# LSTM stage of a fused network kernel: one semaphore increment for two gates, input products four steps apart, more fillers ahead of the loop, and fillers on a 64x64 part of the array

## The reference, cut to what matters

```python
t = t + _L1_ffn_ref(_ln_t(t), ...)

def _L1_ffn_ref(x, U_i, V_i, b_i, U_f, V_f, b_f, U_c, V_c, b_c, U_o, V_o, b_o):
    B, T, _ = x.shape                       # 4, 256, 64
    xi = xt @ U_i + b_i                     # also xf, xg, xo
    def step(carry, xs):
        h, c = carry
        i_t = sigmoid(xi_t + h @ V_i)       # f_t is computed but not used below
        g_t = tanh(xg_t + h @ V_c)
        o_t = sigmoid(xo_t + h @ V_o)
        c_new = h * c + i_t * g_t
        h_new = o_t * tanh(c_new)
        return ((h_new, c_new), h_new)
```

## Time and profile before

| What | Value |
|---|---|
| Median of 3 runs | 818.9 us (811.82 to 820.67) |
| The profiled execution | 824.19 us |
| Its span, first to last instruction | 822.4 us |
| Mean granted TensorE clock | 0.80 of 2.4 GHz |
| TensorE matmul busy | 779.4 us (95%), fillers included |
| VectorE, ScalarE, GpSimd busy | 348.6, 231.5 and 123.0 us |

### The profile page before, as it was taken

One profiled execution on the slowest core, in us unless ns is written; L12 is line 12 of the kernel. 1 busy time (PEld: TensorE's weight loads), 2 busy tenths in 40 slices (PEclk: granted clock), 3 DMA queues, 4 the chain that ended last, 5 costly groups with the idle time before them and its releaser, 6 DMA issues.

```text
span 822.4 us, 17334 instructions
## 1 busy us (share of the span) xinstructions
PE 779.4 (95%) x7035; PEld 447.1 (54%) x7035; DVE 348.6 (42%) x1245; ACT 231.5 (28%) x1136; POOL 123.0 (15%) x148
## 2 busy tenths in 40 slices
PE   6898999999999999999898979999999999999998
PEld 3555555666556665555323745555555555555554
DVE  3444444433443334454655053444444444444443
ACT  2322222222222222213650012333333333333332
POOL 3333333333332223320000000000000000000000
PEclk8566666555655556658999987999999999999999
DMA  7000000000000000000000000000000000000000
GB/s 262 8 1 2 1 1 0 0 0 0 0 0 0 0 0 0 0 0 1 1 0 1 1 1 2 2 2 2 2 2 2 2 2 2 2 3 2 2 2 14
DMA packets 2994, 6.62 MB, mean 8 GB/s; under 512 B 1649, under 2 KB 2294, under 8 KB 2806
## 3 DMA queue, kind: packets, MB, share of 16 engines
q1 hardware_dynamic: 2934, 5.79, 2.1%
HBM read 5.52 MB, written 0.26 MB: 7 GB/s over the span
## 4 chain that ended last, share of the span: by engine, by line
PE 89%; DVE 8%; issue 1%; POOL 1%; ACT 1%; DVEq 0%; POOLq 0%; ACTq 0%
PE bk L668 26%; PE bk L315 15%; PE bk L648 11%; PE bk L427 4%; PE bk L606 3%; DVE a0y L923 2%; PE bk L642 2%; PE bk L534 2%; PE bk L437 2%; PE bk L552 2%; PE bk L379 2%; DVE hv L921 1%; PE bk L455 1%; PE bk L311 1%; PE bk L460 1%
## 5 line engine op out<-in xcount | busy, mean ns | idle before, releaser
L668 PE MATMUL bk<-idle 128*64 128x512 bf16 (+1 forms) x975 | 235.7, 363 | 0.0
L315 PE MATMUL bk<-idle 128*128 128x256 bf16 x608 | 147.3, 397 | 2.1 <-POOL lrcur L265 2.1
L648 PEld LDWEIGHTS bk<-mem,lvh 64*64 64x64 f32 x3072 | 80.9, 134 | 88.0 <-DVE mem L1093 83.7
L668 PEld LDWEIGHTS bk<-idle 128*64 128x64 bf16 x975 | 87.2, 110 | 57.7 <-issue 2.7
L1090 DVE TENSOR_TENSOR_SCAN bk<-gx 128x16 f32<-128x16 f32 x256 | 51.0, 199 | 131.9 <-ACT gx L820 131.9
L648 PE MATMUL bk<-mem,lvh 64*64 64x4 f32 x3072 | 103.4, 204 | 0.0
L820 ACT ACTIVATE gx<-bk 128x8 f32<-128x8 f32 x256 | 47.1, 184 | 178.1 <-PE bk L648 178.1
L315 PEld LDWEIGHTS bk<-idle 128*128 128x128 bf16 x608 | 67.4, 129 | 42.6 <-issue 11.5
L1093 DVE SCALAR_TENSOR_TENSOR mem<-og,bk 128x4 f32<-128x4 f32 x256 | 40.6, 158 | 57.4 <-ACT bk L824 57.4
L281 POOL TENSOR_TENSOR mem<-mem,gcur 128x1024 f32<-128x1024 f32 x16 | 30.3, 1892 | 212.6 <-DVE mem L950 212.3
L824 ACT ACTIVATE bk<-bk 128x4 f32<-128x4 f32 x256 | 40.4, 158 | 52.8 <-DVE bk L1090 52.0
(11 more groups left out here) (274 smaller groups left out, 857.3 us busy)
## 6 DMA issues: line engine op xcount, KB each, us to landing
cw<-in_cw SPq DMA_DIRECT2D x1, 3456.0 KB, 11.2
w<-in_w SPq DMA_DIRECT2D x2, 512.0 KB, 3.6
xs<-in_x SPq DMA_DIRECT2D x1, 256.0 KB, 2.6
out<-xs SPq DMA_DIRECT2D x1, 256.0 KB, 2.1
memw<-in_memw SPq DMA_DIRECT2D x1, 128.0 KB, 2.1
lu<-in_lu SPq DMA_DIRECT2D x1, 97.5 KB
wqkv<-in_wqkv SPq DMA_DIRECT2D x1, 96.0 KB, 2.2
lv<-in_lv SPq DMA_DIRECT2D x1, 96.0 KB
```

Source lines behind the costliest of these rows:

```text
L315: nc.tensor.matmul(bk[:, bank, 0:256], idle[:, 0:128], idle[:, 128:128 + 256], start=True, stop=True)
L648: return nc.tensor.matmul(bk[HALF[n], 3 * (s // CH % 2) + g, c:c + B], lvh[HALF[k], g, :], hist[HALF[k], s, :], start=False, stop=True, sk ...
L668: nc.tensor.matmul(bk[0:D, 7, 0:n], idle[:, 0:D], idle[:, 128:128 + n], start=True, stop=True)
```

## The change

What it does:

- TensorE signals gates_ig once per step, after the second of the two gates, and ScalarE waits for s + 1 in place of 2s + 2.
- The input products of the next chunk are issued in steps 2, 6 and 10 of a chunk in place of 2, 3 and 4. Such a step has two fillers of 512 columns and none of 256.
- The fillers between the steps use 64 rows by 64 output columns in place of 128 rows by 64.
- 39 fillers in place of 28 ahead of the transposes of xn, and six more (`AFTER[8]`, into bank 7) behind them.
- One signal after all eight transposes. VectorE copies bank 4 and ScalarE bank 5, the first half of the steps first; the loop starts when the first half is there, and the second half is waited for at chunk 7, step 2, ahead of the input products for chunk 8.

```diff
+INPUT_STEPS = (2, 6, 10)
...
-AFTER = (8, 14, 10, 4, 0, 20, 4, 28)
+AFTER = (8, 14, 10, 4, 0, 20, 4, 39, 6)
...
             busy(AFTER[7], 0)
             pe.wait_ge(sem("ln"), 3)
-            for n in range(NT):
-                ins = nc.tensor.transpose(bk[0:D, 4 + n // 4, (n % 4) * 128:(n % 4 + 1) * 128], xn[:, n, :], ident[:, :])
-                if n % 4 == 3:
-                    ins.then_inc(sem("t3T_ps"), 1)
+            for c in range(2):
+                for b in range(B):
+                    ins = nc.tensor.transpose(bk[0:D, 4 + b // 2, (b % 2 * 2 + c) * 128:(b % 2 * 2 + c + 1) * 128], xn[:, 2 * b + c, :], ident[:, :])
+            ins.then_inc(sem("t3T_ps"), 1)
+            busy(AFTER[8], 7)
             pe.wait_ge(sem("ld_l"), 32)
-            pe.wait_ge(sem("t3T"), 3)
+            pe.wait_ge(sem("t3T_a"), 1)
+            pe.wait_ge(sem("t3T_v"), 2)
...
                 recurrent(s, 0, 0, 0)
-                recurrent(s, 0, 0, 1).then_inc(sem("gates_ig"), 1)
+                recurrent(s, 0, 0, 1)
                 recurrent(s, 1, 1, 0)
                 recurrent(s, 1, 1, 1).then_inc(sem("gates_ig"), 1)
...
-                if 2 <= s % CH < 5 and s // CH + 1 < S // CH:
-                    inputs_part(s // CH + 1, s % CH - 2)
-                    fills = max(fills - 1, 0)
+                last = FILL_LAST
+                if s % CH in INPUT_STEPS and s // CH + 1 < S // CH:
+                    if (s // CH + 1) * CH == S // 2:
+                        pe.wait_ge(sem("t3T_a"), 2)
+                        pe.wait_ge(sem("t3T_v"), 3)
+                    inputs_part(s // CH + 1, INPUT_STEPS.index(s % CH))
+                    fills, last = FILL - 1, 0
                 if s + 1 < S:
-                    for n in [FILL_N] * fills + [FILL_LAST]:
-                        nc.tensor.matmul(bk[0:D, 7, 0:n], idle[:, 0:D], idle[:, 128:128 + n], start=True, stop=True)
+                    for n in [FILL_N] * fills + [last] * (last > 0):
+                        nc.tensor.matmul(bk[0:D, 7, 0:n], idle[0:D, 0:D], idle[0:D, 128:128 + n], start=True, stop=True)
...
             table(ACT.Tanh)
+            act.wait_ge(sem("t3T_ps"), 1)
+            for c in range(2):
+                nc.scalar.copy(
+                    t3T[0:D, c * 128:(c + 1) * 128, 2:4].rearrange("p s b -> p b s"),
+                    bk[0:D, 5, :].rearrange("p (b c s) -> p b c s", b=2, c=2)[:, :, c, :]).then_inc(sem("t3T_a"), 1)
...
-                act.wait_ge(sem("gates_ig"), 2 * s + 2)
+                act.wait_ge(sem("gates_ig"), s + 1)
...
-            for n in range(2):
-                dve.wait_ge(sem("t3T_ps"), n + 1)
-                for c in range(2):
-                    ins = nc.vector.tensor_copy(
-                        t3T[0:D, c * 128:(c + 1) * 128, 2 * n:2 * n + 2].rearrange("p s b -> p b s"),
-                        bk[0:D, 4 + n, :].rearrange("p (b c s) -> p b c s", b=2, c=2)[:, :, c, :])
-                ins.then_inc(sem("t3T"), 1)
+            dve.wait_ge(sem("t3T_ps"), 1)
+            for c in range(2):
+                nc.vector.tensor_copy(
+                    t3T[0:D, c * 128:(c + 1) * 128, 0:2].rearrange("p s b -> p b s"),
+                    bk[0:D, 4, :].rearrange("p (b c s) -> p b c s", b=2, c=2)[:, :, c, :]).then_inc(sem("t3T_v"), 1)
```

More of the change, by code:

```diff
@@ L1008, in _ @@
             nc.vector.tensor_copy(sel.rearrange("p (e m) -> p e m", e=E), wide(pick3[:, :], 128)).then_inc(sem("sel"), 1)
-            nc.vector.memset(t3T[D:D + 1, :, :], 1.0).then_inc(sem("t3T"), 1)
+            nc.vector.memset(t3T[D:D + 1, :, :], 1.0).then_inc(sem("t3T_v"), 1)
             dve.wait_ge(sem("ld_l"), 32)
```

## The result

The changed kernel takes 961.39 us (median of 4 runs, 958.39 to 965.46) against 819.78 us for the kernel before (4 runs): a ratio of 1.1754, 95% interval 1.1666 to 1.1842. It is slower by 17.5%, far outside the forecast range of 798 to 816. Some executions are a few us slower than the rest, whatever the kernel: ratios leave these out, medians do not.

The account below looks back on a forecast made before the run. The prediction took the chain of dependences to set ordinary steps and TensorE's queue the input steps, with a half-clock dip at the loop's start. Terms -0.7 - 6.9 - 4.6 = -12.2 took 818.9 to 806.7 us, range 798 to 816.

Parts of the forecast that it names:

- Fillers on 64x64. They stream the same columns: cost 0: Between the steps: fillers on 64 rows by 64 columns take the same time as 128-row ones, 0 us.
- the clock is lost with the quadrant: In the loop: 64-row fillers may not hold full clock; +228 us, about 1045 (about 930 if alternating); chance 0.11.
- The dip, -6.9: Start of the LSTM loop: with TensorE kept occupied, the 15.61 us at half clock become 8.69, so -6.9 us.
- the first rival: In the opening: the clock falls all the same, as transposes and small products do not keep it; 813.9 us, chance 0.14.
- The opening, -0.7: Ahead of the loop: copies and input products finish earlier, first recurrent products at 487.85 instead of 488.57, -0.7 us.
- The input steps, -4.6: 42 input steps at full clock: losing the 256-column filler saves 0.11 us each, 1.24 instead of 1.35, -4.6 us.
- One increment, 0: Weight load to ScalarE in each step: one semaphore increment in place of two, at most 0.04 us a step, taken as 0.
- The border between shapes: Filler to recurrent product: 0.12 us beyond what the columns need, removed if both are 64x64, only widening slack in ordinary steps.
- the last rival: Input steps cost more by the change of array shape, +0.12 us in each of 45, at most +5.4; 812.1 us, chance 0.08.

## Why the prediction was wrong, step by step

**"Fillers on 64x64. They stream the same columns: cost 0"** is the step that failed: the term of 0 measured +163 us done alone (979.38 against 816.71). The argument looked only at streamed columns and at the border between shapes; that a filler's work is to hold the clock was left to a rival with a chance of 0.11. Two things were missed in a row: the clock fell, and at half clock fillers sized for full clock outlast the chain of dependences. With this term undone the kernel takes 806.65, so the other terms can be read from the runs with full clock.

**The rival "the clock is lost with the quadrant"** is what happened: half level from 474.6 to the end. The argument that spoke against it, that fillers on half of the columns hold the clock, was true and did not bear on it: 32 columns with all rows held it too, and 128 columns with half of the rows did not. Its price, about 1045 (its own terms give 1047), was too high by 84, mostly because it took the half-clock step of 2.16 from the earlier trace rows, of the 128-row fillers, while that with 64x64 fillers is 1.87. Another way to split the loss is more useful: half clock 23 us, fillers in the queue 143.

**The dip, -6.9**, was right. In the changed kernel and in the opening alone the clock stays full through the opening, so the first rival, that transposes and small products would not keep it, did not come true here. By the opening alone, 7.3 us less the 1.26 and plus the 0.4 of the next paragraph, it was worth about 6.5.

**The opening, -0.7**, was mis-sized: from xn to the first recurrent products 2.95 us in place of 4.21, so -1.26, mainly because the six input products took 0.7 us (470.86 to 471.56) and not the 1.1 taken from input steps. A first step of 1.64 us in place of 1.24 gives 0.4 of it back.

**The input steps, -4.6**, were right by the trace: 1.24 us in place of 1.35 in the part alone. The medians do not show it.

**One increment, 0**, was wrong in size: 0.024 us a step, some 6 us over the loop. That ScalarE "waits for the later of the two increments in any case" does not exclude a price. The trace agrees with what the Trainium skill says ("TensorE: Matmul & The Clock Gate", The cost: per-tile semaphore tail), 26.3 ns for an increment, though its increments follow one another directly and these are two products apart.

**The border between shapes**, the 0.12 us that the prediction read there, is not isolated. With 64x64 fillers a half-clock step is 0.28 us shorter and an input step at full clock 0.03. That agrees with the drain of which the Trainium skill speaks ("TensorEngine Tiling (Array Packing)", Key Properties), but the half-clock number also holds the overlap named above, and 128x32 fillers, which have the border too, bring the input step to 1.23 by themselves. No rise of the input steps came, which answers the last rival. That an ordinary step at full clock gains nothing from it was right; the chain of dependences sets it.

That 806.65 met 806.7 so closely is partly chance. In the traces, from the end of xn to the last gate, the kernel with 128-row fillers has 315.3 us (487.96 to 803.28) against 332.8, so 17.5 less and not 12.2: the increment and the opening made up most of the rest. The ratio of 0.9778 on the forecast's 818.9 gives 801, not 806.7: inside the range, with the gain forecast for these parts some 5 us too low. Medians move by several us with the stretch ahead of the loop.

## What to carry to other kernels

A filler's price is the time by which it holds up the work behind it, but its worth is the clock that it holds: before changing its shape, ask which row of a trace shows that shape holding the level, and where there is none, weigh the loss of the clock over the whole stretch against the few hundredths of a microsecond to be won. Here the wanted shape could be had by feeding both row halves at the same time: 798.65 us, 2.5% under the kernel before (0.9694 to 0.9803), where the changed kernel lost 17.5%. Most of these 2.5% come from the other parts of the change, which give 2.2% with 128-row fillers. And fillers sized to end just ahead of a dependence at full clock stand in its way at half clock, so that a lost clock cost six times more through them than by itself.

## What the runs showed of the hardware that was not expected

- Level of the clock in the loop, by filler: 128x64 and 128x32 and two 64x64 at the same time, full; 64x64 with 1792 or 2048 columns, 64x128, and 64x64 in turn on two quadrants, half, each from a few us into the loop or earlier to its end. TensorE was recorded busy for the whole of the half-clock stretches with fillers, so a full busy line does not say that the clock is held. Other counts of rows, the upper rows alone, and other data than zeros were not tried.
- Without fillers a step at half clock is 1.31 us, only 0.09 over that at full clock (1.22), and that kernel is 1.3% over the kernel before (ratio 0.9992 to 1.0267): most of the chain is ScalarE, VectorE and the hops between engines.
- TensorE does not start its matmuls strictly in the order of the queue: at half clock, with 64x64 fillers, half of the recurrent records started beside a filler and 0.39 us ahead of one queued before them (601.67 and 602.06), in every step from 500 us on. With fillers of 128x64 or 64x128 all twelve stayed behind.
- One semaphore increment fewer on TensorE shortened the step by 0.024 us although another came later.
- The first step of the loop takes 1.64 to 1.67 us at full clock in all kernels with the new opening; its scan on VectorE starts 0.46 us after ScalarE is done (472.17 to 472.63 in the changed kernel). Why is not settled.
